# Cross attention: text columns in quarters, a shift row among the projections, casts on POOL

## The chip, the core and the metric

The kernel runs on one core of a Trainium2 chip. A time is the device time of one execution in microseconds (us). Engines: PE (TensorE: matmuls), DVE (VectorE), ACT (ScalarE), POOL (GpSimd), and SP, whose queue issues the transfers.

## What is computed

One decoder layer, post-normalised, in float32, for 4 batches of 256 text tokens of width 512: self attention, cross attention, and a feed-forward layer with adapters. The change touches the cross attention alone. Its keys and values come from 1601 context tokens and the batch's 256 text tokens; 16 query heads of width 96 share 4 key/value heads.

```
hidden = concatenate([context, latents], axis=1)          # (4, 1857, 512)
q = (latents @ Wq.T)...;  k = (hidden @ Wk.T)...;  v = (hidden @ Wv.T)...
attn = softmax(einsum('bkgqd,bksd->bkgqs', q, k) / sqrt(96))
out = einsum('bkgqs,bksd->bkgqd', attn, v) @ Wo.T
x = layernorm(x + out)
```

## The kernel before

Every float32 operand of a matmul is split in two: a high part, rounded to the matmul's format, and a low part, the remainder. A product is three matmuls (`PARTS`: high-high, high-low, low-high). So each operand costs a copy that rounds (the high part, mostly ACT) and a subtraction (the low part, DVE or POOL).

`cross_attention` handles the batches one after the other. Each engine walks the same list of steps (`schedule_b`) and does its share of each; semaphores order the engines among each other. Within an engine the order is that of the list.

*The head of a batch* (`projection_steps`) turns `hidden` into keys and values, in seven chunks of columns: six of 256 context columns and the last with 66 of the context and the 256 text columns. For each chunk SP loads four quarters of 128 partitions into `hraw` (`load_chunk`, L1014), ACT makes the high part (L1004), POOL the low part (L1287). PE projects three key tiles (L1083, `k`) and two or three value tiles (L1087, `v`), 12 matmuls each: four quarters c of the width 512, times three parts. Four PSUM banks take the results in turn; ACT and DVE empty them (L1182 and L1186, L1240 and L1244). The last chunk's text columns come already split from DRAM (L1018): the transfer is issued once the chunk that held the buffer before, chunk 4, is projected, and PE waits for it at the last chunk's first key tile.

*The shift.* Before the softmax of a group, the largest score of each query is estimated by eight coarse matmuls (`coarse`, L1103; step `max`) into one PSUM buffer, which DVE reduces (L1251); four steps go over the first 1024 keys and four over the rest. The negated maxima (L1254) are transposed by PE into a row (`shift_row`, L1114), which ACT copies into an extra row of the queries (L1193). For the first group these steps stand among the projections: the table `before` puts them ahead of a tile, `behind` after one.

*Attention* (`attention_steps`): eight groups per batch, two per key/value head, of eight steps j each. A step is up to six score matmuls (L1132), the exponential on ACT (L1202), the high part on ACT (L989), the low part on DVE (L995), and, two steps later, up to six value matmuls (L1145). The eighth step of a group is half as long: three score matmuls of 65 rows. Each step also takes one coarse maximum of the next group. A group's result is divided by its sums on POOL (L1294, tile `b_y`), once per group, at j = 4 of the next.

Some preparation lies inside these groups: the queries of the next key/value head (step `queries`, groups 2 and 4: high part ACT L1174, low part POOL L1298, 96x1024), and the first two chunks of the next batch (step `hidden` marked `next`, groups 3 and 5: high part ACT L1004, low part POOL L1287), both at j = 6.

```
if g in (2, 4) and j == 6:
    s += [("queries", g // 2 + 1)]
if g in (3, 5) and j == 6:
    s += [("hidden", g // 2 - 1, "next")]
```

Of the kernel before, what the change touches and what calls it, by code (L numbers as in the profile page):

```python
# [28 lines left out]
HI, LO = 0, 1  # L29
# [803 lines left out]
def projection_steps(ahead):  # L833

    last = len(CHUNKS) - 1
    proj = projections()
    before = {x: i for i, x in enumerate([("v", 4, t) for t in TILES_OF_CHUNK[4]] + [("k", 5, 0), ("k", 5, 2)])}
    behind = {("v", 5, TILES_OF_CHUNK[5][0]): 4, ("v", 5, TILES_OF_CHUNK[5][1]): 5,
# [15 lines left out]
def attention_steps():  # L854

    s = []
    for k in range(STEPS):
        g, j = divmod(k, PAIRS)
        more = g + 1 < GROUPS
        if more and j == 0:  # L860
            s += [("max", g + 1, 0)]
        step = [("scores", k)] + [("pv", k - 2)] * (k >= 2)
        s += step if j else step[::-1]
        if more and j == PAIRS - 1:
            s += [("row", g + 1)]
        if more and j < PAIRS - 1:
            s += [("max", g + 1, j + 1)]
        if g and j == 3:
            s += [("sums", g - 1)]
        if g and j == 4:  # L870
            s += [("spread", g - 1)]
        if g in (2, 4) and j == 6:
            s += [("queries", g // 2 + 1)]
        if g in (3, 5) and j == 6:
            s += [("hidden", g // 2 - 1, "next")]
    return s + [("split", STEPS - 1)]
# [21 lines left out]
def cross_attention(nc, idf, edges, ctx_t, w_kv, hraw, hid_mem, hid, xt_dram, q_dram, q_out, y_dram, y_out, last_loads):  # L898
# [8 lines left out]
    with ExitStack() as st:  # L907
# [29 lines left out]

        h_in, text_in = sem("b_h_in", 16 * C * NCH), sem("b_text_in", 16)
        h_hi, h_lo = sem("b_h_hi", NCH), sem("b_h_lo", NCH * C)
# [38 lines left out]
        def run(e, handle):  # L978

            for step, b in schedule_b():  # L980
                handle(step, b)

        def high_part(act, b, k):

# [22 lines left out]
        def _(sp):  # L1007
            def load_chunk(b, j, low_done):
# [6 lines left out]
                if own < n:  # L1015

                    sp.wait_ge(full.sem, full.at(b, max(k for k, p in enumerate(proj) if p[1] == j - 2) + 1))
                    sp.dma_start(f(hid[:, j % 2, :, :, own:n]), xt_dram[:, :, :, b * T:(b + 1) * T]).then_inc(text_in.sem, 16)  # L1018

# [45 lines left out]
        def _(pe):  # L1065
            def project(k, b):
                kind, j, i = proj[k]
                c0, n = CHUNKS[j]
                if (kind, i) == ("k", 0):
                    pe.wait_ge(h_hi.sem, h_hi.at(b, j + 1))  # L1070
                    if j == NCH - 1:
                        pe.wait_ge(text_in.sem, text_in.at(b, 16))
                if k >= 4:
# [4 lines left out]
                for c in range(C):  # L1078
                    if (kind, i) == ("k", 0):
                        pe.wait_ge(h_lo.sem, h_lo.at(b, j * C + c + 1))  # L1080
                    for a, m in PARTS:
                        if kind == "k":
# [67 lines left out]
            def handle(step, b):  # L1150
                kind, *arg = step
                todo = {"proj": project, "max": coarse, "row": shift_row, "scores": scores, "pv": values}
                if kind in todo:
                    todo[kind](*arg, b)
# [4 lines left out]
        def _(act):  # L1159
            act.sem_inc(h_hi.sem, 1)  # L1160
            act.sem_inc(exp_done.sem, 2)
            act.sem_inc(o_out.sem, 1)

            def handle(step, b):
                kind, *arg = step
                if kind == "hidden":
                    split_hidden(act, b, arg[0])
                elif kind == "queries":
                    kv = arg[0]
                    act.wait_ge(q_in.sem, q_in.at(b, 16 * (kv + 1)))  # L1170

                    if kv >= 2:
                        act.wait_ge(s_made.sem, s_made.at(b, (kv - 1) * 2 * PAIRS))
                    act.activation(q[0:HD2, kv % 2, HI, :], qraw[:], ACT.Copy).then_inc(q_hi.sem, 1)  # L1174
                elif kind == "proj":
                    k = arg[0]
                    what, j, i = proj[k]
                    c0, n = CHUNKS[j]
                    act.wait_ge(full.sem, full.at(b, k + 1))
                    if what == "k":  # L1180
                        for dst, src in key_parts(i, bank_of(k), c0, n):
                            s = act.activation(dst[HI], src, ACT.Copy)  # L1182
                        s.then_inc(kv_hi.sem, 1)
                    else:
                        rows = KT2[i][1]
                        act.activation(v[0:rows, HI, i, :, 0:HD2],  # L1186
                                       bank_of(k)[0:rows, 0:KV2 * HD2].rearrange("p (h d) -> p h d", h=KV2), ACT.Copy)\
                           .then_inc(kv_hi.sem, 1)
                elif kind == "row":
# [3 lines left out]
                    act.activation(q[ROWB:ROWB + 1, kv % 2, HI, hp * BANK:(hp + 1) * BANK], ps_x[0:1, :], ACT.Copy)\  # L1193
                       .then_inc(row_made.sem, 1)
                elif kind == "scores":
                    k = arg[0]
# [76 lines left out]
        def _(pool):  # L1273
# [6 lines left out]
            def handle(step, b):  # L1280
                kind, *arg = step
                if kind == "hidden":
                    j = arg[0]
                    n = from_context(j)
                    pool.wait_ge(h_hi.sem, h_hi.at(b, j + 1))
                    for c in range(C):
# [8 lines left out]
                elif kind == "queries":  # L1295
                    kv = arg[0]
                    pool.wait_ge(q_hi.sem, q_hi.at(b, kv + 1))
                    pool.tensor_tensor(q[0:HD2, kv % 2, LO, :], qraw[:], f(q[0:HD2, kv % 2, HI, :]), ALU.subtract)\  # L1298
# [325 lines left out]
```

## Time and profile before

| | us |
|---|---|
| three runs: median (lowest to highest) | 1933.54 (1930.08 to 1937.99) |
| the profiled execution: time / span | 1935.04 / 1933.2 |
| PE matmul busy, of the span | 1874.4 (97%) |
| DVE / ACT / POOL busy | 1229.7 / 1184.8 / 654.3 |
| attention matmuls, L1145 and L1132, busy | 376.2 and 374.8 |
| projection matmuls, L1083 and L1087, busy | 130.0 and 133.0 |
| coarse matmuls, L1103, busy | 152.5 |

The span runs from the first to the last instruction; the rest of the 1935.04 lies around it. The granted clock of PE is 0.99 of its full speed over the span. Matmuls are pipelined and a matmul's end is modelled, so a stall of PE shows some tenths of a microsecond shorter than it is. In a timeline row, the bracket at the end gives the idle time of the engine before the instruction and who ended it; "issue" means that the profile shows no releaser. The cross attention of the first batch starts before 780 us, its attention groups at about 815, and the second batch's at about 1081.

### The profile page before, as it was taken

The page shows a single profiled execution, that of the slowest core. Times are in us where ns is not written, and L with a number is a line of the kernel's source. Part 1 is how long each engine was busy: PE and PEld are TensorE (multiplying, and loading weights), DVE is VectorE, ACT ScalarE, POOL GpSimd, SP SyncE. Part 2 cuts the span into 40 slices and gives each one's busy share as a digit, 9 for nine tenths or more (in the row PEclk, how much of TensorE's full clock was granted, in tenths as well). Part 3 has the DMA queues.
Part 4 walks back from the last instruction along what each step waited for, and adds up shares of the span by engine and source line. Part 5 has one row for each costly group of instructions (what it writes and reads, how often), then busy time and mean ns, then how long its engine had stood idle before and what let it go on. Part 6 is the DMA issues. An engine that isn't in the chain of part 4 may idle for free. (4 is left out here: it accounts for less than half of the span.)

```text
span 1933.2 us, 28030 instructions
## 1 busy us (share of the span) xinstructions
PE 1874.4 (97%) x9512; PEld 1542.0 (80%) x9512; DVE 1229.7 (64%) x2123; ACT 1184.8 (61%) x2081; POOL 654.3 (34%) x682
## 2 busy tenths in 40 slices
PE   7999999999999999999999999999999999999798
PEld 5888888888888788877779877788777798777576
DVE  4665656566566712577865678745778656787654
ACT  5666656666566633467775577764677755777620
POOL 5666757667576522101103011121011030110341
PEclk8999999999999999999999999999999999999899
DMA  4001101001010354100102000111001023000220
GB/s 170 28 28 28 48 11 49 27 27 43 11 54 13 114 193 126 55 5 17 28 20 79 11 9 27 28 39 55 5 17 28 20 77 133 9 17 9 90 82 27
DMA packets 59384, 89.84 MB, mean 46 GB/s; under 512 B 7060, under 2 KB 42260, under 8 KB 58518
## 3 DMA queue, kind: packets, MB, share of 16 engines
q1 hardware_dynamic: 59288, 88.57, 14.5%
q8 instruction: 59, 0.97, 0.2%
q14 instruction: 37, 0.30, 0.1%
HBM read 67.52 MB, written 21.03 MB: 46 GB/s over the span
## 5 line engine op out<-in xcount | busy, mean ns | idle before, releaser
L1145 PE MATMUL b_o_ps<-b_pr,b_v 128*97 128x512 f32 (+1 forms) x1440 | 376.2, 395 | 12.0 <-DVE b_pr L995 10.7
L1132 PE MATMUL b_s<-b_q,b_kt 97*128 97x512 f32 (+1 forms) x1440 | 374.8, 394 | 2.0 <-DVE b_v L1244 2.0
L1251 DVE TENSOR_REDUCE b_mx<-b_m 128x1 f32<-128x1024 f32 (+1 forms) x256 | 286.7, 1120 | 120.6 <-PE b_m L1103 119.3
L995 DVE TENSOR_TENSOR b_pr<-b_pf,b_pr 128x1024 fp32r<-128x1024 f32 (+1 forms) x256 | 310.1, 1211 | 67.6 <-ACT b_pr L989 67.6
L1202 ACT ACTIVATE b_pf<-b_s 128x1024 f32<-128x1024 f32 (+1 forms) x256 | 247.5, 967 | 135.8 <-PE b_s L1132 135.3
L1145 PEld LDWEIGHTS b_o_ps<-b_pr,b_v 128*97 128x97 f32 (+1 forms) x1440 | 231.8, 162 | 111.8 <-ACT b_pr L989 12.1
L1132 PEld LDWEIGHTS b_s<-b_q,b_kt 97*128 97x128 f32 (+1 forms) x1440 | 262.7, 185 | 64.6 <-issue 3.7
L1294 POOL TENSOR_TENSOR b_y<-b_recs,b_o 96x512 f32<-96x512 f32 x32 | 41.3, 1290 | 768.7 <-ACT b_recs L1217 768.7
L989 ACT ACTIVATE b_pr<-b_pf 128x1024 fp32r<-128x1024 f32 (+1 forms) x256 | 257.5, 1006 | 42.0 <-PE b_o_ps L1145 38.5
L445 PE MATMUL a_ring<-a_xt,w_a 128*128 128x512 f32 x1128 | 278.9, 398 | 0.0
L445 PEld LDWEIGHTS a_ring<-a_xt,w_a 128*128 128x128 f32 x1128 | 208.8, 191 | 41.0
L495 PE MATMUL a_ring<-a_wo,a_y 128*128 128x512 f32 x768 | 191.2, 398 | 0.0
L800 POOL TENSOR_TENSOR a_p<-a_p,a_rec 128x128 f32<-128x128 f32 (+1 forms) x256 | 130.5, 530 | 143.3 <-DVE a_rec L704 143.3
L495 PEld LDWEIGHTS a_ring<-a_wo,a_y 128*128 128x128 f32 x768 | 140.2, 189 | 29.2 <-DVE a_y L714 1.0
L1103 PE MATMUL b_m<-b_kt,b_q 96*128 96x512 f32 (+1 forms) x512 | 152.5, 379 | 1.8 <-DVE b_mx L1251 1.8
L1083 PE MATMUL b_s<-a_hid,w_kv 128*128 128x256 f32 (+1 forms) x1008 | 130.0, 286 | 6.8 <-issue 4.9
L1083 PEld LDWEIGHTS b_s<-a_hid,w_kv 128*128 128x128 f32 x1008 | 127.8, 189 | 9.4 <-issue 5.7
L605 ACT ACTIVATE a_p<-a_ms,a_top 128x128 f32<-128x128 f32 (+1 forms) x256 | 114.2, 448 | 31.0 <-DVE a_top L698 29.4
L1087 PE MATMUL b_s<-w_kv,a_hid 128*128 128x384 f32 (+1 forms) x720 | 133.0, 337 | 0.0
L698 DVE CUSTOM_DVE_ANT_0 a_ms<-a_s,a_mask 128x128 f32<-128x128 f32 (+1 forms) x256 | 81.1, 354 | 80.3 <-PE a_s L462 80.0
L1287 POOL TENSOR_TENSOR a_hid<-hraw,a_hid 128x256 fp32r<-128x256 f32 (+1 forms) x108 | 75.7, 732 | 165.0 <-ACT a_hid L1004 165.0
L1087 PEld LDWEIGHTS b_s<-w_kv,a_hid 128*128 128x128 f32 (+1 forms) x720 | 123.6, 184 | 3.3
(117 smaller groups left out, 2615.6 us busy)
## 6 DMA issues: line engine op xcount, KB each, us to landing
hraw<-in_ctx_t SPq DMA_DIRECT2D x92, 128.0 KB, 2.4
raw_a<-in_w_qkv SPq DMA_DIRECT2D x30, 384.0 KB, 3.3
raw_a<-in_w_o SPq DMA_DIRECT2D x32, 256.0 KB, 3.1
queries<-a_q SPq DMA_DIRECT2D x24, 256.0 KB, 2.0
b_qraw<-queries SPq DMA_DIRECT2D x16, 384.0 KB, 4.0
attended<-b_y SPq DMA_DIRECT2D x32, 192.0 KB, 2.1
c_yraw<-attended SPq DMA_DIRECT2D x3, 1536.0 KB, 7.3
x_t<-a_xt SPq DMA_DIRECT2D x2, 2048.0 KB, 8.2
```

The source lines that it names most:

```text
L445: mm = pe.matmul(bank[:], w[:, a, c, t * HD:(t + 1) * HD], xt[:, m, c, n * HALF:(n + 1) * HALF], start=i == 0, stop=i == 3 * C - 1)
L495: mm = pe.matmul(bank[:], y[:, b % 2, a, h, tt * P:(tt + 1) * P], wo[:, m, h, :], start=i == 0, stop=i == 3 * GRP - 1)
L800: pool.tensor_tensor(seen, seen, rec[:, h, qt:qt + 1].to_broadcast([P, (qt + 1) * P]), ALU.mult)\
L989: act.activation(pr[0:rows, k % 2, HI, 0:n], pf[0:rows, k % 2, 0:n], ACT.Copy).then_inc(p_hi.sem, 1)
L995: dve.tensor_tensor(pr[0:rows, k % 2, LO, 0:n], pf[0:rows, k % 2, 0:n], f(pr[0:rows, k % 2, HI, 0:n]), ALU.subtract).then_inc(p_lo.sem, 1)
L1083: mm = pe.matmul(bank[:, 0:n], w_k[:, a, c, i * P:(i + 1) * P], hid[:, j % 2, m, c, 0:n], start=s == 0, stop=s == 3 * C - 1)
L1087: mm = pe.matmul(bank[0:rows, 0:KV2 * HD2], hid[:, j % 2, a, c, t0 - c0:t0 - c0 + rows], w_v[:, m, c, :], start=s == 0, stop=s == 3 * C - 1)
L1103: mm = pe.matmul(ps_m[:, x:min(x + BANK, n)], q[0:HD2, kv % 2, HI, hp * BANK + t * P:hp * BANK + (t + 1) * P], kt[0:HD2, HI, kv, c0 + x:c0 ...
L1132: mm = pe.matmul(ps_s[k % 2][0:rows, i * BANK:(i + 1) * BANK], kt[:, a, kv, t0:t0 + rows], q[:, kv % 2, m, hp * BANK:(hp + 1) * BANK], sta ...
L1145: mm = pe.matmul(ps_o[0:HD2 + 1, :], v[0:rows, a, t, g // 2, :], pr[0:rows, k % 2, m, i * BANK:(i + 1) * BANK], start=t == 0 and s == 0, s ...
L1202: act.activation(pf[0:rows, k % 2, 0:n], ps_s[k % 2][0:rows, 0:n], ACT.Exp, scale=SCALE_B)\
L1251: dve.reduce_max(mx[:, g % 2, t, half:half + 1], ps_m[:, 0:MAXW[half][1]], X).then_inc(mx_made.sem, 1)
```

## The change

Four edits in `cross_attention` and its schedule:

- The text columns come in four transfers, one per quarter c, with a semaphore each. PE waits for quarter c ahead of its three matmuls of the last chunk's first key tile.
- The first four maxima stand one tile earlier or so: ahead of the second key tile of chunk 4, both value tiles of chunk 4 and the second key tile of chunk 5. The first shift row is issued by PE inside the last value tile, ahead of the last three of its twelve matmuls; ACT copies the row first and that tile's high part second.
- The later query splits (key/value heads 2 and 3) have their high part made by POOL, ahead of the low part, and stand at j = 1 of groups 2 and 4. POOL waits for the queries' transfer and for the last scores that read the buffer.
- The next batch's first two chunks have their high part made by POOL too, still at j = 6 of groups 3 and 5.

```
-    before = {x: i for i, x in enumerate([("v", 4, t) for t in TILES_OF_CHUNK[4]] + [("k", 5, 0), ("k", 5, 2)])}
+    before = {x: i for i, x in enumerate([("k", 4, 1)] + [("v", 4, t) for t in TILES_OF_CHUNK[4]] + [("k", 5, 1)])}
...
-        if g in (2, 4) and j == 6:
-            s += [("queries", g // 2 + 1)]
+        if g in (2, 4) and j == 1:
+            s += [("queries", g // 2 + 1, "spare")]
         if g in (3, 5) and j == 6:
-            s += [("hidden", g // 2 - 1, "next")]
+            s += [("hidden", g // 2 - 1, "spare", "next")]
...
-                    sp.dma_start(f(hid[:, j % 2, :, :, own:n]), xt_dram[:, :, :, b * T:(b + 1) * T]).then_inc(text_in.sem, 16)
+                    for c in range(C):
+                        sp.dma_start(f(hid[:, j % 2, :, c, own:n]), xt_dram[:, :, c, b * T:(b + 1) * T]).then_inc(text_in[c].sem, 16)
...
-                    if j == NCH - 1:
-                        pe.wait_ge(text_in.sem, text_in.at(b, 16))
...
                         pe.wait_ge(h_lo.sem, h_lo.at(b, j * C + c + 1))
+                        if j == NCH - 1:
+                            pe.wait_ge(text_in[c].sem, text_in[c].at(b, 16))
+                    if (k, c) == (NP - 1, C - 1):
+                        shift_row(0, b)
...
                     act.activation(q[ROWB:ROWB + 1, kv % 2, HI, hp * BANK:(hp + 1) * BANK], ps_x[0:1, :], ACT.Copy)\
                        .then_inc(row_made.sem, 1)
+                    if g == 0:
+                        project_high(NP - 1, b)
...
+                    if spare(arg):
+                        pool.wait_ge(h_in.sem, h_in.at(b, 16 * C * (j + 1)))
+
+                        pool.wait_ge(full.sem, full.at(b, 0))
+                        pool.tensor_copy(hid[:, j % 2, HI, :, 0:n], hraw[:, :, 0:n]).then_inc(h_hi.sem, 1)
...
+                    if spare(arg):
+                        pool.wait_ge(q_in.sem, q_in.at(b, 16 * (kv + 1)))
+
+                        pool.wait_ge(s_made.sem, s_made.at(b, (kv - 1) * 2 * PAIRS))
+                        pool.tensor_copy(q[0:HD2, kv % 2, HI, :], qraw[:]).then_inc(q_hi.sem, 1)
```

PE, chunks 4 to 6 of a batch (256 columns: key tiles of a context chunk; 384: value tiles; 322: key tiles of the last chunk; `b_m`: a maximum). Before:

```order
L1083 MATMUL b_s<-a_hid,w_kv 128x256 x36
L1103 MATMUL b_m<-b_kt,b_q 128x512 x2
L1087 MATMUL b_s<-w_kv,a_hid 128x384 x12
L1103 MATMUL b_m<-b_kt,b_q 128x512 x2
L1087 MATMUL b_s<-w_kv,a_hid 128x384 x12
L1103 MATMUL b_m<-b_kt,b_q 128x512 x2
L1083 MATMUL b_s<-a_hid,w_kv 128x256 x24
L1103 MATMUL b_m<-b_kt,b_q 128x512 x2
L1083 MATMUL b_s<-a_hid,w_kv 128x256 x12
L1083 MATMUL b_s<-a_hid,w_kv 128x322 x36
```

and now:

```order
L1090 MATMUL b_s<-a_hid,w_kv 128x256 x12
L1110 MATMUL b_m<-b_kt,b_q 128x512 x2
L1090 MATMUL b_s<-a_hid,w_kv 128x256 x24
L1110 MATMUL b_m<-b_kt,b_q 128x512 x2
L1094 MATMUL b_s<-w_kv,a_hid 128x384 x12
L1110 MATMUL b_m<-b_kt,b_q 128x512 x2
L1094 MATMUL b_s<-w_kv,a_hid 128x384 x12
L1090 MATMUL b_s<-a_hid,w_kv 128x256 x12
L1110 MATMUL b_m<-b_kt,b_q 128x512 x2
L1090 MATMUL b_s<-a_hid,w_kv 128x256 x24
L1090 MATMUL b_s<-a_hid,w_kv 128x322 x36
```

Three maxima in place of two now stand ahead of chunk 4's last value tile, and one in place of two between that tile and the 322-column tiles.

PE, the end of a batch's head (`b_x`: the shift row; `b_q,b_kt`: scores). Before:

```order
L1087 MATMUL b_s<-w_kv,a_hid 128x384 x12
L1114 MATMUL b_x<-b_idr,b_neg 1x128 x4
L1103 MATMUL b_m<-b_kt,b_q 128x512 x2
L1132 MATMUL b_s<-b_q,b_kt 128x512 x6
L1103 MATMUL b_m<-b_kt,b_q 128x512 x2
```

and now:

```order
L1094 MATMUL b_s<-w_kv,a_hid 128x384 x9
L1121 MATMUL b_x<-b_idr,b_neg 1x128 x4
L1094 MATMUL b_s<-w_kv,a_hid 128x384 x3
L1110 MATMUL b_m<-b_kt,b_q 128x512 x2
L1139 MATMUL b_s<-b_q,b_kt 128x512 x6
L1110 MATMUL b_m<-b_kt,b_q 128x512 x2
```

The row's four transposes went ahead of the last three matmuls of the last value tile.

POOL, the attention groups of a batch that is not the last (`b_y`: one per group; `CAST`: the new copies). Before:

```order
L1294 TENSOR_TENSOR b_y<-b_recs,b_o 96x512 x2
L1298 TENSOR_TENSOR b_q<-b_qraw,b_q 96x1024
L1294 TENSOR_TENSOR b_y<-b_recs,b_o 96x512
L1287 TENSOR_TENSOR a_hid<-hraw,a_hid 128x256 x4
L1294 TENSOR_TENSOR b_y<-b_recs,b_o 96x512
L1298 TENSOR_TENSOR b_q<-b_qraw,b_q 96x1024
```

and now:

```order
L1308 TENSOR_TENSOR b_y<-b_recs,b_o 96x512
L1315 CAST b_q<-b_qraw 96x1024
L1317 TENSOR_TENSOR b_q<-b_qraw,b_q 96x1024
L1308 TENSOR_TENSOR b_y<-b_recs,b_o 96x512 x2
L1298 CAST a_hid<-hraw 128x4x256
L1301 TENSOR_TENSOR a_hid<-hraw,a_hid 128x256 x4
L1315 CAST b_q<-b_qraw 96x1024
L1317 TENSOR_TENSOR b_q<-b_qraw,b_q 96x1024
```

The query split moved ahead of a `b_y`, and a cast stands ahead of each split; between a `b_y` and the hidden split nothing else stands on POOL.

## Rows read from the trace of the kernel before

**Rows 1.** The page, part 1: busy time (share of the span), instructions

```profile
PE 1874.4 (97%) x9512; PEld 1542.0 (80%) x9512; DVE 1229.7 (64%) x2123; ACT 1184.8 (61%) x2081; POOL 654.3 (34%) x682
```

**Rows 2.** Timeline of POOL, groups 1 to 4 of the first batch: start, length, what

```profile
855.30 1.29 POOL L1294 TENSOR_TENSOR b_y<-b_recs,b_o 96x512 f32<-96x512 f32 x1 [60.05 <-ACT b_recs L1217]
...
879.89 1.30 POOL L1294 TENSOR_TENSOR b_y<-b_recs,b_o 96x512 f32<-96x512 f32 x1 [23.30 <-ACT b_recs L1217]
...
885.51 2.41 POOL L1298 TENSOR_TENSOR b_q<-b_qraw,b_q 96x1024 fp32r<-96x1024 f32 x1 [4.32 <-ACT b_q L1174]
...
905.76 1.29 POOL L1294 TENSOR_TENSOR b_y<-b_recs,b_o 96x512 f32<-96x512 f32 x1 [17.84 <-ACT b_recs L1217]
...
930.61 1.29 POOL L1294 TENSOR_TENSOR b_y<-b_recs,b_o 96x512 f32<-96x512 f32 x1 [15.45 <-ACT b_recs L1217]
```

**Rows 3.** Timeline, all engines, end of group 2 of the first batch

```profile
884.39 1.04 ACT L1174 ACTIVATE b_q<-b_qraw 96x1024 fp32r<-96x1024 f32 x1
...
885.04 0.86 PE L1132 MATMUL b_s<-b_q,b_kt 97*65 97x512 f32 x3
...
886.41 2.58 DVE L995 TENSOR_TENSOR b_pr<-b_pf,b_pr 128x1024 fp32r<-128x1024 f32 x1
...
889.15 1.60 PE L1145 MATMUL b_o_ps<-b_pr,b_v 128*97 128x512 f32 x6 [1.09 <-DVE b_pr L995]
```

**Rows 4.** The same, end of group 1, which holds no split

```profile
856.34 1.33 DVE L995 TENSOR_TENSOR b_pr<-b_pf,b_pr 128x1024 fp32r<-128x1024 f32 x1 [0.38 <-ACT b_pr L989]
...
858.53 1.21 DVE L995 TENSOR_TENSOR b_pr<-b_pf,b_pr 128x1024 fp32r<-128x1024 f32 x1
...
860.45 0.86 PE L1132 MATMUL b_s<-b_q,b_kt 97*65 97x512 f32 x3
...
861.15 1.55 PE L1145 MATMUL b_o_ps<-b_pr,b_v 128*97 128x512 f32 x6
...
861.79 1.22 DVE L995 TENSOR_TENSOR b_pr<-b_pf,b_pr 128x1024 fp32r<-128x1024 f32 x1
...
863.28 1.54 PE L1145 MATMUL b_o_ps<-b_pr,b_v 128*97 128x512 f32 x6
```

**Rows 5.** Timeline of PE: last chunk's key tiles, first and fourth batch

```profile
797.00 5.60 PE L1083 MATMUL b_s<-a_hid,w_kv 128*128 128x322 f32 x36 [0.80 <-issue]
...
1595.98 5.60 PE L1083 MATMUL b_s<-a_hid,w_kv 128*128 128x322 f32 x36 [1.97 <-issue]
```

**Rows 6.** Timeline of SP's queue, end of the first batch's loads

```profile
791.02 0.61 SPq L1018 DMA_DIRECT2D a_hid<-x_t  x1
...
794.43 1.76 SPq L1014 DMA_DIRECT2D hraw<-in_ctx_t  x4
```

**Rows 7.** DMA issues of that stretch: count, KB each, us to landing

```profile
hraw<-in_ctx_t SPq DMA_DIRECT2D x4, 128.0 KB, 2.7
```

**Rows 8.** Timeline of PE in the first batch's head, the second maximum

```profile
788.16 0.73 PE L1103 MATMUL b_m<-b_kt,b_q 96*128 96x512 f32 x2 [0.44 <-DVE b_mx L1251]
```

**Rows 9.** Timeline, all engines, from the first shift row on

```profile
814.23 0.16 DVE L1254 TENSOR_REDUCE b_neg<-b_mx 128x4 fp32r<-128x8 f32 x1
...
814.53 0.41 PE L1114 MATMUL b_x<-b_idr,b_neg 128*1 128x128 f32 x4
...
814.66 0.49 ACT L1186 ACTIVATE b_v<-b_s 128x384 fp32r<-128x384 f32 x1 [1.99 <-PE b_s L1087]
...
815.18 0.58 ACT L1193 ACTIVATE b_q<-b_x 1x512 fp32r<-1x512 f32 x1
...
815.18 0.56 DVE L1244 TENSOR_TENSOR b_v<-b_s,b_v 128x384 fp32r<-128x384 f32 x1 [0.80 <-ACT b_v L1186]
...
815.66 1.21 DVE L1251 TENSOR_REDUCE b_mx<-b_m 128x1 f32<-128x1024 f32 x1
...
815.97 1.63 PE L1132 MATMUL b_s<-b_q,b_kt 97*128 97x512 f32 x6 [0.51 <-DVE b_v L1244]
...
817.44 0.63 PE L1103 MATMUL b_m<-b_kt,b_q 96*128 96x512 f32 x2
```

More of the change, by code:

```diff
@@ L936, in cross_attention @@
         const_made, edges_in, late_in = sem("b_const_made"), sem("b_edges_in"), sem("b_late_in")
-        h_in, text_in = sem("b_h_in", 16 * C * NCH), sem("b_text_in", 16)
+        h_in, text_in = sem("b_h_in", 16 * C * NCH), [sem(f"b_text_in{c}", 16) for c in range(C)]
         h_hi, h_lo = sem("b_h_hi", NCH), sem("b_h_lo", NCH * C)
@@ L981, in run, with spare @@
                 handle(step, b)
+        def spare(arg):
+            return arg[-1] == "spare"
         def high_part(act, b, k):
@@ L1152, in handle @@
                 todo = {"proj": project, "max": coarse, "row": shift_row, "scores": scores, "pv": values}
-                if kind in todo:
+                if kind in todo and step != ("row", 0):
                     todo[kind](*arg, b)
@@ L1162, in _, with project_high @@
             act.sem_inc(o_out.sem, 1)
+            def project_high(k, b):
+                what, j, i = proj[k]
+                c0, n = CHUNKS[j]
+                act.wait_ge(full.sem, full.at(b, k + 1))
+                if what == "k":
+                    for dst, src in key_parts(i, bank_of(k), c0, n):
+                        s = act.activation(dst[HI], src, ACT.Copy)
+                    s.then_inc(kv_hi.sem, 1)
+                else:
+                    rows = KT2[i][1]
+                    act.activation(v[0:rows, HI, i, :, 0:HD2],
+                                   bank_of(k)[0:rows, 0:KV2 * HD2].rearrange("p (h d) -> p h d", h=KV2), ACT.Copy)\
+                       .then_inc(kv_hi.sem, 1)
             def handle(step, b):
                 kind, *arg = step
-                if kind == "hidden":
+                if kind == "hidden" and not spare(arg):
                     split_hidden(act, b, arg[0])
-                elif kind == "queries":
+                elif kind == "queries" and not spare(arg):
                     kv = arg[0]
                     act.wait_ge(q_in.sem, q_in.at(b, 16 * (kv + 1)))
-                    if kv >= 2:
-                        act.wait_ge(s_made.sem, s_made.at(b, (kv - 1) * 2 * PAIRS))
                     act.activation(q[0:HD2, kv % 2, HI, :], qraw[:], ACT.Copy).then_inc(q_hi.sem, 1)
                 elif kind == "proj":
[L1176 to L1188, printed above, removed]
+                    if arg[0] < NP - 1:
+                        project_high(arg[0], b)
                 elif kind == "row":
```

## The prediction

> **What bounds the kernel.** The page comes first: TensorE is busy for 97% of the span, the other engines for 64% at most [rows 1]. So only time in which PE stands still can be won, some 59 us, and the cross attention holds little of it, in short stalls. Next I read POOL's timeline for the rhythm of a batch: one multiplication into b_y per group, the same point of each group, so two starts give the length of a group [rows 2]. A plain group takes 879.89 - 855.30 = 24.59 us. The group with a query split takes 905.76 - 879.89 = 25.87, 1.28 more; the group with a split of the next batch's hidden chunk 930.61 - 905.76 = 24.85, 0.26 more.
>
> The timeline at the end of such a group says why [rows 3]. PE's last three score matmuls start at 885.04. ACT's copy of the queries ends at 885.43 and POOL's subtraction runs from 885.51 to 887.92 [rows 2]. DVE's subtraction is due at 886.41, takes 2.58 and ends at 888.99: 1.07 after POOL's end. Without a POOL instruction it takes 1.22 [rows 4], and behind the b_y multiplication, which ends at 855.30 + 1.29 = 856.59, the same thing shows: issued 856.34, ended 857.67, 1.08 after POOL. So a running POOL instruction shuts this DVE subtraction out, and the value matmuls, which follow its end by 0.16, are late. ACT's extra copy is not the cause: the subtraction is issued 1.37 after the scores' start with it and 1.34 without. The place is tender, since the matmuls at 863.28 need a subtraction that ended only at 863.01; in the step before, one that ends at 859.74 is needed at 861.15 [rows 4].
>
> In the head of a batch I read PE's stalls: at the first key tile of the last chunk, 0.80 in the first batch to 1.97 in the fourth, and 0.2 more that the modelled end of the matmul before hides [rows 5]; at one maximum, 0.44 [rows 8]; at the first scores, 0.51 [rows 9].
>
> **The splits on POOL.** Taken away: 8 query splits on ACT (two per batch) at 1.28 and 6 hidden splits at 0.26, together 11.8 us of PE's time. Put in: a cast on POOL ahead of the same subtractions. POOL waits for no order of ACT's, only for semaphores, so the place in the schedule says little. The queries of kv 2 are let go when the scores of step 15 end, 860.45 + 0.86 = 861.31; with the 0.08 from ACT's end to POOL's start in [rows 2, 3] the cast starts at 861.39, 0.4 ahead of the DVE subtraction of 861.79. For a cast of c us, that subtraction ends at 861.39 + c + 1.07 and the matmuls start 0.16 later: at 862.62 + c in place of 863.28. The stall is c - 0.66.
>
> No row has a one-input POOL instruction of this size. Its ends are ACT's copy of the same tile, 1.04 [rows 3], and POOL's subtraction of it, 2.41. POOL's 512 elements take 1.29 and 1024 take 2.41 [rows 2]: 1.12 per 512, 0.17 fixed. With one stream to read in place of two I halve the slope: c = 1.29, nearest to ACT's row, and the stall is 0.63 (ends 0.38 and 1.75). It falls on 5 query splits: kv 2 of four batches, and kv 3 of the last. In the first three batches kv 3 stands in POOL's queue behind the hidden split, which is still running when its scores end, so its cast comes after the tender place; I cost it at nothing. If that cover is gone it is 3 x 0.63. The POOL subtraction behind each cast meets the next, smaller DVE subtraction, after which PE has two score steps ahead of it: nothing.
>
> The Trainium skill (GPSIMD Engine Reference, section 4.1 Engine selection) rates one-input elementwise work on GpSimd at about line rate; with its 1.03 cycles per element at 1.2 GHz (section 3.1) c would be an estimated 1.06 and the sum below 1.2 us better. No row here shows it.
>
> The hidden splits now start straight behind the b_y multiplication. DVE's waiting subtraction goes first, to 857.67; the cast runs to 858.96; DVE's, due at 858.53, ends at 860.03, in time for 861.15. POOL's four subtractions of 256 elements, 0.73 each by that slope, then run from 860.03; the third ends at 862.22, and DVE's of 861.79 ends at 863.29: matmuls 0.17 late. It may be 0 to 0.73 by phase. Six times 0.17 is 1.0. Sum of the part: 11.8 - 5 x 0.63 - 1.0 = **7.6 saved**. ACT's lost copies save nothing more, since nothing waited for them, and SP only loads later queries earlier.
>
> **The text in quarters.** In the first batch the transfer is issued at 791.02 [rows 6] and PE goes on at 797.00, 5.98 later, having stood from 796.0. Its 36 matmuls take 5.60, so a tile of 12 takes 1.8 and the 3 of one quarter 0.45 [rows 5]. Four transfers on the same queue overlap: four of 128 KB are issued within 1.76 [rows 6] and land 2.7 after their own issue [rows 7]. I take it that the last quarter lands when the whole did; then only 3 matmuls are left behind it. One maximum, 0.63 less the hidden 0.2 [rows 9], now stands ahead of the issue that stood behind it. So the tile ends 1.8 - 0.45 - 0.43 = 0.92 sooner, in four batches **3.7 saved**. The ends: nothing, if the last quarter lands 0.9 later than the whole; the whole wait, 1.0 in the first batch and 2.2 in the last, about 6 in all, if none is left.
>
> **The maxima** move one place forward. The wait of 0.44 is for DVE's reduction of the maximum before, which stands among the subtractions of the key tiles; those keep their number, so the wait moves to the next maximum. 0, between -0.4 and +0.4 a batch.
>
> **The first shift row** goes ahead of the last 3 of the 12 matmuls. It can't start before DVE's negation ends at 814.39, and before, the 12 matmuls ended at about that time, ACT's copy of them starting at 814.66 [rows 9]. So PE now waits with 3 of them left, an estimated 0.5 by the 0.15 for 322 columns [rows 5], and these run behind the row. ACT makes the row when its transposes end, 814.53 + 0.41, 0.2 sooner, since its copy of v, 0.49, now comes second; the scores could start at 815.77, not 815.97. But what is queued behind: the 3 matmuls end near 815.5, ACT's copy of v near 816.07, DVE's subtraction of v, 0.56, near 816.6 in place of 815.74, and the reduction behind it, 1.21, near 817.8 in place of 816.87. PE's second maximum, at 817.44 before, waits for that and starts at 817.87. **0.43 lost** a batch, 1.7 in all; it may be 0.2 won instead.
>
> **Sum.** 7.6 + 3.7 - 1.7 = 9.6 saved. The profiled execution took 1935.04, so 1925.4; it lies 1.5 above the median of the runs, 1933.54, against which I state 1923.9.
>
> **Rivals.**
> - The cast is as slow as POOL's subtraction, 2.41. Then 5 x 1.75, and a hidden split late by an estimated 0.7 (0.16 at 861.15 and a whole piece of POOL's behind it), 6 x 0.7: 12.95 against 11.8. Sum 1.1 - 3.7 + 1.7 = -0.9: 1932.6. For it speaks that every POOL row of this size is slow; against it, that all of them read two tiles. The Trainium skill (Perfetto Trace Analysis, section Optimizing Scalar/DVE Operations) warns that work moved between GpSimd and DVE may not help, since they share a read port. The rows agree on the sharing; here the work comes from ACT.
> - The row's place does no harm, because PE's second maximum waits for something else anyway: 0.2 won a batch. Sum -7.6 - 3.7 - 0.8 = -12.1: 1921.4.
> - A one-input cast doesn't shut DVE out. Then only the 1.0 of the hidden subtractions stays: -10.8 - 3.7 + 1.7 = -12.8: 1920.7. Every overlap in the rows is with a two-input POOL instruction, so it is open.
> - Slower: the quarters go one after the other. The whole took 5.98, 128 KB take 2.7, so 256 KB about 3.2, and the last lands 12.6 after the first issue. The first tile then ends at 0.43 + 12.6 + 0.45 = 13.5 against 5.98 + 1.8 = 7.8: 5.7 a batch, some 21 in all, as the later batches waited longer before, the last by 1.2. Sum -7.6 + 21 + 1.7 = +15: 1948.6. The kernel becomes slower once the last quarter lands some 9 after the first issue. Against it speak [rows 7].
>
> **Chances.** What a measurement of this kernel can tell is about 0.5%, 9.7 us, and the forecast sits on that bound. Forecast 57%, the slow cast 18%, the harmless row 12%, the free port 8%, the serial quarters 5%. Half of the forecast and nearly all of the second and third rivals give faster by over 0.5%: 0.48. Slower: 0.05. Within: 0.47. The range runs from 1917 (both good rivals together, and less waiting for the text) to 1933, which takes in the slow cast's sum.
>
> **What will show it.** POOL's cast rows: near 1.3, or near 2.4. DVE's subtraction at the end of group 1: 2.1 if shut out by a cast of 1.3, 1.2 if the port is free. b_y to b_y: about 25.2 in the group with kv 2, 24.6 to 24.8 with a hidden split. The first 322-column matmuls: a short wait for the last quarter only. PE at the second maximum after the row: a wait of about 0.6 for DVE. The forecast is wrong if a cast starts at another point than right behind the last scores, or if the head's gain is taken back by a wait that I don't list.

## The result, and the profile after

| | before | changed |
|---|---|---|
| median of 6 runs each (lowest to highest), us | 1933.86 (1930.08 to 1937.99) | 1923.22 (1921.13 to 1927.1) |
| ratio of the two, 95% interval | | 0.9944 (0.9931 to 0.9956) |
| the profiled execution: time / span, us | 1935.04 / 1933.2 | 1923.49 / 1921.7 |

The kernel became 0.56% faster: 1923.2 against the 1923.9 forecast, inside the range. The same kernel measured once more (e7) gave 1924.93, ratio 0.9943 (0.9926 to 0.9959). The sizes of the single terms agree less well, and part of the 10.6 us is not the edits' doing; both are worked out below.

Where the time went is read by cutting a batch at fixed instructions and adding up four batches. "Text and maxima" runs from chunk 4's first key tile to the last chunk's first value tile, "row" from there to the fourth maximum of the next group, "groups" from the first to the sixth b_y. The sums are worked out from starts in the timelines of PE and POOL; the first value of a cell is the first batch.

| stage | before | changed | sum of four |
|---|---|---|---|
| opening: start of the first batch's chunk 4 | 780.71 | 776.51 | -4.2 |
| text and maxima | 21.73, 21.70, 22.32, 22.89 | 21.97, 20.90, 21.83, 21.83 | -2.1 |
| row | 20.32, 20.33, 20.31, 20.31 | 20.81, 20.82, 20.81, 20.82 | +2.0 |
| groups | 126.05, 126.06, 126.04, 125.31 | 124.13, 124.13, 124.10, 123.70 | -7.4 |

The edited stages give -7.5; the opening, which no edit touches, -4.2: together 11.7, where the span lost 11.5. The page of the changed kernel, part 1, against [rows 1]: ACT lost 9.6 us of work, POOL took on 27.1 (part of it waiting, as its rows below show), PE is the bound as before.

```profile
PE 1871.0 (97%) x9512; PEld 1538.3 (80%) x9512; DVE 1233.9 (64%) x2123; ACT 1175.2 (61%) x2067; POOL 681.4 (35%) x696
```

**The splits.** POOL's timeline of the changed kernel, groups 1 to 4 of the first batch, the answer to [rows 2]:

```profile
851.83 1.29 POOL L1308 TENSOR_TENSOR b_y<-b_recs,b_o 96x512 f32<-96x512 f32 x1 [60.77 <-ACT b_recs L1226]
857.97 1.03 POOL L1315 CAST b_q<-b_qraw 96x1024 fp32r<-96x1024 f32 x1 [4.86 <-PE b_s L1139]
859.09 3.25 POOL L1317 TENSOR_TENSOR b_q<-b_qraw,b_q 96x1024 fp32r<-96x1024 f32 x1
876.89 1.30 POOL L1308 TENSOR_TENSOR b_y<-b_recs,b_o 96x512 f32<-96x512 f32 x1 [14.55 <-ACT b_recs L1226]
901.48 1.30 POOL L1308 TENSOR_TENSOR b_y<-b_recs,b_o 96x512 f32<-96x512 f32 x1 [23.29 <-ACT b_recs L1226]
902.71 2.05 POOL L1298 CAST a_hid<-hraw 128x1024 fp32r<-128x1024 f32 x1
904.84 3.79 POOL L1301 TENSOR_TENSOR a_hid<-hraw,a_hid 128x256 fp32r<-128x256 f32 x4
908.58 2.03 POOL L1315 CAST b_q<-b_qraw 96x1024 fp32r<-96x1024 f32 x1
...
926.44 1.30 POOL L1308 TENSOR_TENSOR b_y<-b_recs,b_o 96x512 f32<-96x512 f32 x1 [13.34 <-ACT b_recs L1226]
```

The groups now last 876.89 - 851.83 = 25.06, 24.59 and 24.96, then 24.52 and 25.00, where they took 24.59, 25.87, 24.85, 25.83 and 24.91. The cast takes 1.03, not 1.29, and starts right behind the last scores, as forecast (0.13 behind their end at 857.84, where the prediction had 0.08). The same place on the other engines, against [rows 4]:

```profile
856.98 0.86 PE L1139 MATMUL b_s<-b_q,b_kt 97*65 97x512 f32 x3
...
858.32 1.77 DVE L999 TENSOR_TENSOR b_pr<-b_pf,b_pr 128x1024 fp32r<-128x1024 f32 x1
...
860.23 1.59 PE L1152 MATMUL b_o_ps<-b_pr,b_v 128*97 128x512 f32 x6 [0.26 <-DVE b_pr L999]
```

The cast ends at 859.00, DVE's subtraction at 860.09, 1.09 later, and PE's value matmuls start 0.14 behind that: the chain of the prediction, with a cast 0.26 quicker. The Trainium skill (GPSIMD Engine Reference, section 4.1 Engine selection) puts one-input work near line rate, and the prediction's estimate with its cycles per element was 1.06 (0.88 + 0.17, so rather 1.05); this trace agrees, with 1.03. The hidden split meets the same place (POOL's fourth subtraction ends at 904.84 + 3.79 = 908.63):

```profile
904.72 1.21 DVE L999 TENSOR_TENSOR b_pr<-b_pf,b_pr 128x1024 fp32r<-128x1024 f32 x1
...
907.91 1.81 DVE L999 TENSOR_TENSOR b_pr<-b_pf,b_pr 128x1024 fp32r<-128x1024 f32 x1
...
909.86 1.36 PE L1152 MATMUL b_o_ps<-b_pr,b_v 128*97 128x512 f32 x5 [0.26 <-DVE b_pr L999]
```

The cast of the hidden split is over at 904.76, so the subtraction due at 904.72 runs free, in 1.21. The next one, due at 907.91, meets POOL's fourth piece and ends at 909.72, again 1.09 after POOL. The cast of kv 3 at 908.58 follows too late to harm, as forecast.

**The text.** SP's queue, and PE and its weight loads, in the changed kernel, first batch, against [rows 5, 6]:

```profile
787.29 2.58 SPq L1023 DMA_DIRECT2D a_hid<-x_t  x4
```

```profile
793.69 4.95 PE L1090 MATMUL b_s<-a_hid,w_kv 128*128 128x322 f32 x30 [0.76 <-DMA a_hid<-x_t]
...
793.66 0.44 PEld L1090 LDWEIGHTS b_s<-a_hid,w_kv 128*128 128x128 f32 x3 [1.00 <-issue]
794.34 4.02 PEld L1090 LDWEIGHTS b_s<-a_hid,w_kv 128*128 128x128 f32 x27 [0.24 <-issue]
```

The four issues take 2.58 in SP's queue, the one transfer of before 0.61. PE waits for the third quarter and again for the last, which is there 794.34 - 787.29 = 7.05 after the first issue; the whole took 5.98. In the other batches it is 6.00, 6.92 and 6.91, where the whole took 5.96, 6.58 and 7.14. The first issue itself comes 787.29 - 776.51 = 10.78 after chunk 4's start, where it came 791.02 - 780.71 = 10.31 after it before: one more maximum stands ahead of it.

**The row.** All engines at the end of the head, against [rows 9]:

```profile
810.27 0.16 DVE L1263 TENSOR_REDUCE b_neg<-b_mx 128x4 fp32r<-128x8 f32 x1
...
810.58 0.40 PE L1121 MATMUL b_x<-b_idr,b_neg 128*1 128x128 f32 x4 [0.44 <-DVE b_neg L1263]
...
811.62 0.49 ACT L1181 ACTIVATE b_v<-b_s 128x384 fp32r<-128x384 f32 x1
...
811.86 1.59 PE L1139 MATMUL b_s<-b_q,b_kt 97*128 97x512 f32 x6
...
812.15 0.56 DVE L1253 TENSOR_TENSOR b_v<-b_s,b_v 128x384 fp32r<-128x384 f32 x1 [1.72 <-ACT b_v L1181]
812.62 1.22 DVE L1260 TENSOR_REDUCE b_mx<-b_m 128x1 f32<-128x1024 f32 x1
...
813.89 0.73 PE L1110 MATMUL b_m<-b_kt,b_q 96*128 96x512 f32 x2 [0.45 <-DVE b_mx L1260]
```

PE waits for the negation ahead of the transposes (0.44), the copy of v comes second on ACT, v's subtraction and the maximum's reduction follow late on DVE, and PE's second maximum now waits for that reduction.

### The profile page after: what moved, and what is told of

It is laid out like the page before. It is cut to its first block and busy times, and to the rows that moved or that the text cites. A ratio compares the mean times of both kernels' runs of the same rounds, so it can differ in the third digit from the quotient of the medians.

```text
span 1921.7 us, 28060 instructions
## 1 busy us (share of the span) xinstructions
PE 1871.0 (97%) x9512; PEld 1538.3 (80%) x9512; DVE 1233.9 (64%) x2123; ACT 1175.2 (61%) x2067; POOL 681.4 (35%) x696
## 5 line engine op out<-in xcount | busy, mean ns | idle before, releaser
L999 DVE TENSOR_TENSOR b_pr<-b_pf,b_pr 128x1024 fp32r<-128x1024 f32 (+1 forms) x256 | 314.6, 1229 | 65.3 <-ACT b_pr L993 65.1
L772 POOL TENSOR_TENSOR a_swapped<-a_swapped,a_sin 128x512 f32<-128x512 f32 x80 | 106.5, 1332 | 52.8 <-ACT a_swapped L585 52.8
```

Of the source, the lines that this page charges most:

```text
L999: dve.tensor_tensor(pr[0:rows, k % 2, LO, 0:n], pf[0:rows, k % 2, 0:n], f(pr[0:rows, k % 2, HI, 0:n]), ALU.subtract).then_inc(p_lo.sem, 1)
```

## The experiments

e1 to e4 are each the kernel before with one of the four edits alone, the lines being those of the diff above. The theory is the prediction's: each edit acts in its own stage and nowhere else.

### e1: the text in quarters, alone

```
-  sp.dma_start(f(hid[:, j % 2, :, :, own:n]), xt_dram[:, :, :, ...])
+  for c in range(C):
+      sp.dma_start(f(hid[:, j % 2, :, c, own:n]), xt_dram[:, :, c, ...])
...
+  if j == NCH - 1:
+      pe.wait_ge(text_in[c].sem, text_in[c].at(b, 16))
```

> The kernel before with the text in quarters and nothing else. Stage read: from chunk 4's first key tile to the last chunk's first value tile, 21.73, 21.70, 22.32 and 22.89 us in the four batches before. Theory: a quarter costs SP 0.65 us to issue and the last one lands 6.0 to 7.1 us after the first issue, no sooner than the whole did; what is won is the rest of the tile, 1.8 - 0.45 us, less what the last quarter lands later. With the landings that the changed kernel shows (7.05, 6.0, 6.9, 6.9) the stage is 21.4, 20.4, 21.3, 21.3, so 4 us won in all. Rival: the quarters themselves win nothing and the gain of the changed kernel in this stage comes from the maxima; then the stage stays within 0.2 of before.

Measured: 1924.19 against 1931.38, one run each. Text and maxima 20.72, 20.68, 20.97, 20.99: -5.3, more than the -4 expected; the other stages as before. The four issues take 2.57 in SP's queue in the first batch, and by the trace's landing times the last quarter is there 6.2, 5.6, 6.4 and 6.5 after the first issue. PE in the first batch of e1 no longer waits at all between the last 24 matmuls of 256 columns and the first 24 of 322:

```profile
790.49 6.98 PE L1088 MATMUL b_s<-a_hid,w_kv 128*128 128x256 f32 x48
```

### e2: the maxima, alone

```
-  [("v", 4, t) for t in TILES_OF_CHUNK[4]] + [("k", 5, 0), ("k", 5, 2)]
+  [("k", 4, 1)] + [("v", 4, t) for t in TILES_OF_CHUNK[4]] + [("k", 5, 1)]
```

> The kernel before with the new places of the first four maxima and nothing else. Theory: the wait of 0.44 us only moves to the next maximum, and the text's issue comes one maximum (0.45) later in PE's program, so the same stage is about 0.45 longer in each batch: 22.2, 22.2, 22.8, 23.3. Rival, what the change is meant for: DVE gets room and the wait shrinks; then the stage is 0.3 to 0.6 shorter than before in each batch.

Measured: 1935.17. Text and maxima 22.15, 22.23, 22.13, 23.44: +1.3 against the first profile of before, +1.6 against the mean of six profiles with the single transfer and the old table (88.34 for four batches, between 87.3 and 88.6, and 89.7 in e5, where PE's granted clock was 0.94 from 1570 to 1600 in the fourth batch). The wait of 0.45 at a maximum is still there, at the third one instead of the second:

```profile
788.78 0.73 PE L1107 MATMUL b_m<-b_kt,b_q 96*128 96x512 f32 x2 [0.45 <-DVE b_mx L1254]
```

What is lost is the transfer's issue, which stands behind one more maximum: in SP's queue it comes 10.79 after chunk 4's start in every batch, in the kernel before 10.31. That is 0.48 a batch, 1.9 in all, and does not depend on when the transfer lands.

### e3: the first shift row, alone

```
+  if (k, c) == (NP - 1, C - 1):
+      shift_row(0, b)
...
+  if g == 0:
+      project_high(NP - 1, b)
```

> The kernel before with the first shift row inside the last value tile and nothing else. Stage read: from the last chunk's first value tile to the fourth maximum of the second group, 20.31 to 20.33 us in each batch before. Theory: 0.49 longer, 20.8, with the first scores 0.15 sooner and a wait of about 0.45 shown at the second maximum for DVE; 2.0 us lost over the four batches. Rival: the loss in the changed kernel comes from the other parts (maxima and text that shift DVE's work); then the stage is 20.2 or less here.

Measured: 1936.72. Row 20.84, 20.84, 20.84, 20.82: +2.1. The first scores start 0.15 sooner (13.38 after the first value tile, not 13.53), but PE then waits 0.45 at the second maximum for DVE, which loses more than that. The rival, that the place does no harm, falls.

### e4: the splits on POOL, alone

```
+  s += [("queries", g // 2 + 1, "spare")]
...
+  s += [("hidden", g // 2 - 1, "spare", "next")]
```

> The kernel before with the splits on POOL and nothing else. Stage read: from the first to the sixth multiplication into b_y of a batch, 126.05, 126.06, 126.04 and 125.31 us before. Theory: the splits alone make what the changed kernel shows there, 124.13, 124.13, 124.10 and 123.70, 7.4 us in all; the heads stay within 0.1 of before. Rival: part of it comes from the other edits; then this stage is 0.3 us or more longer than in the changed kernel. For all four: the time ahead of the first batch's chunk 4, which no edit touches, was 780.71 before and 776.51 after; if that is the clock of the first stage it scatters here without regard to the edits, and if it is the change's work it follows them.

Measured: 1923.97. Groups 124.13, 124.13, 124.13, 123.62: -7.45, the whole of what this stage gains in the changed kernel.

### e5: a longer cast

e4 with the queries' high part made by a two-input instruction on POOL, qraw plus zero.

```
-  pool.tensor_copy(q[0:HD2, kv % 2, HI, :], qraw[:])
+  zero = f(v[0:HD2, LO, 0, 0, HD2:HD2 + 1]).to_broadcast([HD2, G2 * T])
+  pool.tensor_tensor(q[0:HD2, kv % 2, HI, :], qraw[:], zero, ALU.add)
...
```

> The splits alone, with the query cast on POOL made by a two-input instruction (queries plus a zero column), so that the high part is the same and the instruction longer. The group with kv 2 took 25.06 us with the cast of 1.03, against 24.59 for a plain group: 0.47 lost. Theory: DVE's subtraction waits for the whole POOL instruction, so each us more costs PE a us: with 2.3 to 2.4 us the group takes 26.3 to 26.45, in all four batches, and the last batch's group with kv 3 26.2 to 26.35; the kv 3 cast that stands behind a hidden split stays free to within 0.3. Rival: only the start of a POOL instruction matters (it goes first and DVE then shares); then these groups stay at 25.1 to 25.3.

Measured: 1930.44 against 1935.62. The group with kv 2 lasts 25.92, between the two expectations, because this instruction took 1.89 and not 2.4, as the timeline of e5 shows:

```profile
857.61 1.89 POOL L1311 TENSOR_TENSOR b_q<-b_qraw,b_v 96x1024 fp32r<-96x1024 f32 x1 [4.84 <-issue]
...
857.96 2.63 DVE L999 TENSOR_TENSOR b_pr<-b_pf,b_pr 128x1024 fp32r<-128x1024 f32 x1
...
860.73 1.60 PE L1149 MATMUL b_o_ps<-b_pr,b_v 128*97 128x512 f32 x6 [1.12 <-DVE b_pr L999]
```

POOL ends at 859.50, DVE at 860.59, 1.09 later. With 1.03 the group lost 25.06 - 24.59 = 0.47, with 1.89 it lost 25.92 - 24.59 = 1.33: 0.86 more cast, 0.86 more stall. So the stall is the cast's duration less 0.56, shown at two durations; the prediction had less 0.66. The last batch's group with kv 3 says the same: 25.79 here, 24.92 in e4. That the cast shuts DVE out is settled; the free port falls, and so does the rival that only POOL's start matters.

### e6: POOL's splits held back three score steps

The changed kernel with the quarters and the casts, but the table and the row of before. The query split waits for three more score steps, the hidden split is listed at j = 1 and waits for three score steps of that same group, 3 or 5.

```
-  pool.wait_ge(s_made.sem, s_made.at(b, (kv - 1) * 2 * PAIRS))
+  pool.wait_ge(s_made.sem, s_made.at(b, (kv - 1) * 2 * PAIRS + 3))
...
-  if g in (3, 5) and j == 6:
+  if g in (3, 5) and j == 1:
...
+  pool.wait_ge(s_made.sem, s_made.at(b - 1, (2 * j + 3) * PAIRS + 3))
```

> Text in quarters and splits on POOL, without the new places of the maxima and of the first shift row, and every POOL split held back until three more score steps of its group are done, so that its instructions fall on steps in which DVE's subtraction has some 2 us of room. Theory: a split's cost is its place alone; all groups then take 24.5 to 24.6 us, so the stage from the first to the sixth b_y is 122.9 in each batch (before 126.05, changed 124.13); chunk 4 to the last chunk's value tile 20.7 to 21.0 as with the quarters alone; sum against before 12.2 + 5.3 = 17.5 us faster, some 10 us faster than the changed kernel. Rival: POOL's longer subtraction meets DVE wherever it stands; then a group with a split stays at 24.9 to 25.1 and the gain over the changed kernel is the 6 us of the head alone.

Measured: 1920.73 (6 runs), ratio 0.9921 (0.9907 to 0.9935). Groups 123.49 each: -9.5, not the 122.9 expected. With text and maxima at -4.0 the stages give -13.5 and the medians -14.9, where -17.5 was expected. The hidden split now costs nothing: the last batch, which has none, shows the same lengths (25.22, 24.28, 25.17, 24.27) as the first (25.23, 24.28, 25.17, 24.24). Each query split still costs about 0.4 over two groups, 25.23 + 24.28 against 24.59 + 24.56 in e8; POOL, DVE and PE in e6 show how:

```profile
870.63 2.40 POOL L1313 TENSOR_TENSOR b_q<-b_qraw,b_q 96x1024 fp32r<-96x1024 f32 x1
871.36 2.75 DVE L999 TENSOR_TENSOR b_pr<-b_pf,b_pr 128x1024 fp32r<-128x1024 f32 x1
874.03 1.01 DVE L1255 TENSOR_REDUCE b_mx<-b_m 128x1 f32<-128x834 f32 x1
875.08 0.70 DVE L1267 STREAM_TRANSPOSE b_recs<-b_o 32x512 f32<-32x512 f32 x1
...
876.73 1.17 DVE L999 TENSOR_TENSOR b_pr<-b_pf,b_pr 128x1024 fp32r<-128x1024 f32 x1
...
878.04 1.60 PE L1150 MATMUL b_o_ps<-b_pr,b_v 128*97 128x512 f32 x6
```

The subtraction due at 871.36 ends at 874.11, 1.08 after POOL's; it pushes the work on the sums, and with it the subtraction of 876.73, whose value matmuls start late, at 878.04.

### e7: the changed kernel once more

No edit.

> The changed kernel once more, beside the kernel before on the same chip. The stages that the edits touch make it 7.5 us faster; the runs shown made it 10.6. Theory: the rest is the opening, where PE's clock comes back some 5 us earlier or later whatever the edits are; with more runs the difference of the medians moves towards 7.5 (0.39%), and the stages repeat to 0.05. Rival: the edits do shorten the opening; then the difference stays at 10 to 11 us and the first batch's chunk 4 starts at 776.5 each time, and at 780.7 in each profile of the kernel before.

Measured: 1924.93 (6 runs). Its profiled execution took 1927.80, with chunk 4 starting at 781.18 where the first profile had 776.51; text and maxima -2.4, row +2.0, groups -7.5. So the opening scatters by 4.7 with the same kernel, and the stages repeat. The difference of the medians stayed at 10.7, which the theory did not expect.

### e8: held back four score steps

e6 with the query split held back by one score step more.

```
-  pool.wait_ge(s_made.sem, s_made.at(b, (kv - 1) * 2 * PAIRS + 3))
+  pool.wait_ge(s_made.sem, s_made.at(b, (kv - 1) * 2 * PAIRS + 4))
```

> As e6, but the query split on POOL is held back by four score steps in place of three. Nothing else differs. Theory (a DVE subtraction that starts while a POOL instruction runs ends about 1.07 after it, and costs PE only what that end passes the next value matmuls' need): the scores of that step end near 871.6 in e6's time base, where DVE's subtraction (due at 871.36) already runs, to 872.6; POOL's cast then waits for it and ends near 873.6, and POOL's subtraction runs 873.7 to 876.1, beside DVE's one-input reduction and transposes and ahead of the subtraction of 876.73. So no DVE subtraction waits: group 2 near 24.6 in place of the pair 25.23 and 24.28 being 0.33 too long, and first to sixth b_y near 122.9 in place of 123.49. Rival (the transposes and the reciprocal of the sums are held up by POOL as well, and with them the sums): the pair stays as long as in e6 or longer, first to sixth b_y 123.5 or more. The comparison with the kernel before again shows whether the difference of medians exceeds the stages' sum (about -14 with the text's share).

Measured: 1915.20 (4 runs), ratio 0.9899 (0.9878 to 0.9920). Groups 122.65, 122.75, 122.67, 122.75: -12.6, and every group between 24.4 and 24.6. POOL, and DVE, in e8:

```profile
872.51 1.76 POOL L1311 CAST b_q<-b_qraw 96x1024 fp32r<-96x1024 f32 x1 [17.45 <-PE b_s L1137]
874.35 2.41 POOL L1313 TENSOR_TENSOR b_q<-b_qraw,b_q 96x1024 fp32r<-96x1024 f32 x1
```

```profile
872.16 1.22 DVE L999 TENSOR_TENSOR b_pr<-b_pf,b_pr 128x1024 fp32r<-128x1024 f32 x1
874.19 1.03 DVE L1255 TENSOR_REDUCE b_mx<-b_m 128x1 f32<-128x834 f32 x1 [0.82 <-PE b_m L1108]
875.25 0.70 DVE L1267 STREAM_TRANSPOSE b_recs<-b_o 32x512 f32<-32x512 f32 x1
...
876.90 1.17 DVE L999 TENSOR_TENSOR b_pr<-b_pf,b_pr 128x1024 fp32r<-128x1024 f32 x1
```

Here the cast waits for DVE's subtraction, not DVE for the cast, and POOL's 2.41 runs beside DVE's reduction and transposes, which take as long as ever. So POOL holds up the subtractions of `b_pr`, and not these, and the rival falls. Two inputs alone don't make the difference: DVE's subtraction of `b_v` reads `b_s`, a PSUM bank, and `b_v`, and in the head of the kernel before it took 0.56 beside a POOL subtraction, as it does without one [rows 9]:

```profile
778.64 2.40 POOL L1298 TENSOR_TENSOR b_q<-b_qraw,b_q 96x1024 fp32r<-96x1024 f32 x1
779.33 0.56 DVE L1244 TENSOR_TENSOR b_v<-b_s,b_v 128x384 fp32r<-128x384 f32 x1 [0.95 <-ACT b_v L1186]
```

Held up in these traces is the DVE instruction whose two inputs both lie in SBUF. The medians differ by 18.1, the stages by 15.6 (text and maxima -3.0); the profiled execution's chunk 4 started at 779.01. This is the fastest kernel of the study. PE's value matmuls sum it up; from the page's groups of the changed kernel, and of e8, the last figures being their idle time:

```profile
L1152 PE MATMUL b_o_ps<-b_pr,b_v 128*97 128x512 f32 (+1 forms) x1440 | 376.1, 394 | 5.0 <-DVE b_pr L999 4.2
```

```profile
L1150 PE MATMUL b_o_ps<-b_pr,b_v 128*97 128x512 f32 (+1 forms) x1440 | 375.6, 394 | 2.2 <-DVE b_pr L999 1.3 <-ACT b_o L1215 0.9
```

### e9 and e10: the kernel before, two more profiles

No edit.

> The kernel before, unchanged, for one more profile. Theory (the opening and the single text transfer scatter from execution to execution, the edited stages do not): start of chunk 4 of the first batch anywhere from 776 to 782; chunk 4 to the last value tile 21.5 to 24.5 per batch, unequal between executions; first to sixth b_y 126.05 and the row's stage 20.3 to within 0.05. Rival (the kernel before has a longer opening than the changed one): 780.7 or more, as in its first profile.

> The same kernel before, for a third profile, with the same expectations: under the theory the start of chunk 4 differs from the other two profiles by up to 5; under the rival it stays within 1 of 780.7.

Measured: 1935.52 and 1929.82, with chunk 4 starting at 781.41 and 776.12; groups and row within 0.05 of the first profile per batch; text and maxima 88.2 and 87.3 for four batches, 88.6 in the first. The rival, a longer opening of the kernel before, falls. The stretches of 2 us that differ are, in the first profile of before (stretch, length, busy time of PE, PEld, DVE, ACT and POOL, then PE's granted clock, the DMA share and GB/s):

```profile
38.00:40.00 2.00, 0.44 (x2) 0.44 (x3) 0.56 (x2) 1.15 (x5) 2.00 (x3) 0.72 0.70 234
40.00:42.00 2.00, 2.00 (x10) 1.98 (x10) 0.87 (x6) 0.12 (x1) 2.00 (x3) 0.50 0.14 56
42.00:44.00 2.00, 2.00 (x6) 1.54 (x5) 1.44 (x5) 1.76 (x6) 1.82 (x4) 0.50 0.05 12
44.00:46.00 2.00, 2.00 (x6) 1.57 (x6) 0.00 (x0) 0.00 (x0) 1.72 (x2) 0.58 0.00 0
```

and in e10:

```profile
38.00:40.00 2.00, 1.08 (x10) 1.08 (x10) 0.69 (x1) 0.00 (x0) 2.00 (x2) 1.00 0.70 203
40.00:42.00 2.00, 2.00 (x11) 1.65 (x10) 1.90 (x6) 1.55 (x6) 2.00 (x3) 1.00 0.02 9
42.00:44.00 2.00, 2.00 (x15) 1.83 (x14) 0.55 (x3) 1.55 (x3) 2.00 (x5) 1.00 0.00 0
44.00:46.00 2.00, 2.00 (x10) 1.62 (x10) 1.77 (x7) 1.58 (x6) 2.00 (x2) 1.00 0.00 0
```

Granted 0.50 is the 1.2 GHz level. In both executions PE had stood still for nearly all of 27 to 29 and of 37 to 39. Behind the second stop PE kept 2.4 GHz in e10; in the first profile it fell to 1.2 GHz and came back before 46. All twelve profiles bear out that the opening goes with this clock and not with the edits. The granted clock from 27 to 47 was 0.66 where chunk 4 started at 780.7 to 781.4 (the first profile, e9, e2, e3, and e7, which is the changed kernel; these five also show 0.89 from 655 to 670, the others 1.00), 0.74 where it started at 779.0 to 779.1 (e6, e8), 0.83 at 776.5 to 776.8 (the changed kernel's first profile, e1, e4, e5), and 0.91 at 776.1 (e10).

## Why the prediction was right, and where not

**Time and sign.** Right, and partly by luck: the terms of the sum came to -9.6, the stages to -7.5 and -7.8 in two profiles of the changed kernel, the medians to -10.6 and -10.7. Of the runs whose mean granted clock is listed, those of equal clock give, before and changed: 0.991, 1936.3 (9 runs) and 1927.8 (1); 0.992, 1934.0 (2) and 1927.6 (3); 0.993, 1933.1 (4) and 1926.0 (1); 0.994, 1932.2 (3) and 1923.1 (3); 0.995, 1930.4 (2) and 1922.5 (1). The differences, 8.5, 6.4, 7.2, 9.1 and 7.8, have a mean of 7.8, which is about what the stages give. The other 3 us go with a higher mean clock in more runs of the changed kernel; why it has them more often, or whether by chance, stays open.

**Splits: -7.6 forecast, -7.4 measured; the mechanism is shown.** ACT's query splits had cost 1.28 to 1.31 each, as read. The stall of a cast, forecast 0.63, was 0.47 (and 0.51 for kv 3 of the last batch: 24.96 where the kernel before had 24.45): c was 1.03 and the formula 0.1 off. The hidden split, forecast to gain 0.26 and lose 0.17, loses: the group of the changed kernel is 24.96 against 24.45 in a plain one of the last batch before, 0.51, and 25.00 against 24.57 at the second place, 0.43, where the kernel before had 0.40 and 0.34. The reading of 0.26 took group 1's 24.59 for a plain group everywhere; at this place a plain one takes 24.45. The step that failed is "the third ends at 862.22, and DVE's of 861.79 ends at 863.29". With the quicker cast everything ran a little sooner: POOL's third piece was done just as DVE's subtraction came due, and the fourth piece got in first. The loss stayed within the 0 to 0.73 by phase. The two errors nearly cancel. The rival of a cast of 2.41 falls with its duration. The Trainium skill's warning in Perfetto Trace Analysis (section Optimizing Scalar/DVE Operations), that work moved between GpSimd and DVE may not help because of a read port that they share, agrees here as far as the sharing goes, 1.08 to 1.09 behind POOL's end wherever a full subtraction of `b_pr` met it; here the work came from ACT. How much of the gain the sharing takes back is a matter of the moment, as e8 gains 5.2 us more in the groups than the change, with the same instructions on the same engines.

**Text: -3.7 forecast, -2.1 and -2.4 measured with the maxima.** Without the extra maximum the prediction's terms are 1.8 - 0.45 = 1.35 a batch, 5.4 in all. The three profiles with quarters and the old table (e1, e6, e8) take 83.4, 84.6 and 85.6, a mean of 84.5 against the 88.3 of the single transfer: 3.8. The step that failed is "I take it that the last quarter lands when the whole did": in the first batch it was there 7.05 after the first issue, not 5.98. By the landing times in the traces, means of four batches, the whole landed 6.0 to 6.3 after its issue in the seven profiles that have it, and the last quarter 6.2 (e1) to 6.6 after the first issue in the five that have quarters: on average 0.3 a batch later. Why stays open. SP's 2.58 for four issues is not enough of a reason, since e1 has the same four and lost nothing. The charge of 0.43 a batch for the maximum ahead of the issue was nearly right: the issue comes 0.48 later, and the stage takes 86.5 and 86.3 in the changed kernel against 84.5.

**Maxima: 0 forecast for their wait, right.** It moved to the next maximum and kept its size, as PE's timeline of the changed kernel shows beside [rows 8]:

```profile
784.44 0.73 PE L1110 MATMUL b_m<-b_kt,b_q 96*128 96x512 f32 x2 [0.45 <-DVE b_mx L1260]
```

**Row: +1.7 forecast, +2.0 measured, shown by e3.** The wait at the second maximum was forecast at 0.6 and is 0.45; the scores start 0.15 sooner, not 0.2. The rival without harm falls.

**Slower, by quarters one after the other:** falls; they overlap, and in the changed kernel the last is there 7.05 after the first issue at most, not 12.6.

Half of the change thus works against the other half: the table and the row cost some 3.6 to 4 us together, by e2, e3 and the stages of the changed kernel; e8 has neither.

## What to carry to other kernels

When work moves to POOL, look first at which DVE instruction that reads two SBUF tiles comes due while it runs; where one does, the work's duration is paid nearly in full (e5). Place it so that DVE's subtraction is already under way and the next one comes after POOL's end. A split that costs nothing there (e8) cost 0.5 us four score steps earlier, with the same instructions. And a wait that a reorder moves does not vanish; follow the engine queue behind it to the next instruction that somebody waits for.

## What was not expected of the hardware

- A DVE subtraction of two SBUF tiles, 128x1024, that comes due while POOL runs ends 1.08 to 1.09 after POOL's end, at every cast of 1.03, at those of 1.89, at a subtraction of 2.40 and at the last of the hidden pieces: nearly its whole free duration of 1.22, as if it had hardly started before. POOL's instructions wait in the same way: the query cast, 1.03 where nothing holds it up, shows 2.03 and 1.76 behind a running subtraction (908.58 in the changed kernel, 872.51 in e8), and ends 0.89 after it both times. So a long POOL row can be a short instruction that waits.
- DVE's reductions and transposes, with one tile to read, took 1.03 and 0.70 beside a running POOL subtraction of 2.41, as without it; its subtraction of `b_v`, with one input in PSUM, 0.56 beside one of 2.40.
- A two-input POOL instruction whose second input is one broadcast column took 1.89 for 96x1024, between the cast's 1.03 and the subtraction's 2.41.
- In the opening PE's clock came back to 2.4 GHz at different points in executions of the same kernel, and the start of chunk 4 moved between 776.12 and 781.41 with it (granted clock 0.91 to 0.66 from 27 to 47): half as much as the change did.
